# Decoder kernel, state-space stage: eight product buffers, scans five groups behind, one buffer of exponent rows loaded in halves, and block-step rows in place of the mask matmul

## Chip, core and metric

One core of one Trainium2 chip. The metric is the device time of the whole kernel in microseconds (us). TensorE is written PE, its weight loads PEld, VectorE DVE, ScalarE ACT, GpSimd POOL and SyncE SP.

## What is computed

A decoder of two layers on x of shape (4, 256, 256) runs in six stages, named A to F in the code: A attention, B a lookup of four experts by token, C a mixture of experts, D the state-space layer, E a second attention, F a second mixture of experts. The change touches stage D alone. With the projection, convolution and gate left out, D computes for each sequence b, each chunk of 128 tokens and each of 64 heads h:

```
dt    = softplus(A_log)
A_cum = cumsum(-dt) within the chunk
L[s, z]  = exp(A_cum[s] - A_cum[z])      for z <= s, else 0
Y_diag[s] = sum_z  (C[s] . B[z]) * L[s, z] * x[z]       8 numbers per head; C and B shared by 8 heads
Y_off     = what the state of the chunk before adds
out   = ((Y_diag + Y_off + D * x / dt) * silu(z_gate)) @ out_proj_w.T
```

## The kernel before

Every engine has its own program, and all five follow one list of steps that `schedule` writes out by hand; an engine skips the kinds of step in which it has no part. Inside an engine the order is fixed, and semaphores tie the engines together.

Stage D works in eight units (4 sequences times 2 chunks, variable `u`). A unit has 16 groups (`hg`, NHG = 16) of four heads each (HG = 4). For one group:

1. PE writes the exponents, 128 x 512 (four heads side by side, z on partitions and s along the row), into one of the three banks of ring AR: line 1450 multiplies the identity by the causal mask `maskt` (-1e30 where s < z), and line 1452 adds A_cum[s] - A_cum[z] by a product of 15 rows (`rows_z`, `rows_s`: each number is split into three bf16 parts).
2. ACT takes the exponential of the bank into a product buffer `M` (line 1055). There are NM = 4 buffers; ACT waits on `m_used` for the buffer to come free.
3. DVE multiplies the buffer by `CBs`, the C.B products, in place (line 1807).
4. PE scans: `scan` multiplies the buffer by the unit's x (line 1114, four matmuls of 32 columns side by side) into a bank of O. PE does this for the group LAG = 3 behind the one whose exponents it writes.

Between the groups the list places other work, by group number: projection of a pair of conv channels (`din`, PE line 1391, ACT lines 983 and 985) at groups 1, 4 and 9 while pairs are left (units 0 to 4), its three `tap` steps on DVE one group apart (line 1749), `th` on ACT (line 996, waits for the taps), `silu` on DVE (line 1759); for the last unit `y_t` (copy ACT 1066, transposes PE 1260, sums on DVE 1833 to 1839), `dy_t` (PE 1484, ACT 1071) and `dy` (PE 1490); for the next unit `at`, `dz` (PE 1397), `zs`, `xt` (PE 1428) and `cb` (PE 1437, DVE copies 1797). `state` stands at group 0. Bank T is one bank with one chain of waits: each user waits until the one before has been read; `at` and `dy_t` both use it.

The exponent rows of a unit come by DMA. At step `at` PE transposes the split sums (`ap_`, line 1418), ACT copies them into AT and, negated, nAT (lines 1030, 1031), and SP issues six DMAs (lines 697, 699) into one of two sets of `rows_s` / `rows_z`, one in the arena and one in `early`, memory that stages A and B used. Before it writes a set again, SP waits for the last group of the unit two back. PE waits for all six before a unit's first group.

Of the kernel before, what the change touches and what calls it, by code (L numbers as in the profile page):

```python
# [367 lines left out]
def decoder(nc, A, out, stages="ABCDEF"):  # L368
    steps = schedule(stages)
    at = number(steps)  # L370
    with ExitStack() as ctx:
# [135 lines left out]
        ap_ = cut(3 * NU * NV // 2, BF16).rearrange("p (u j m g) -> p u j m g", u=NU, j=HG, m=3)  # L507
# [4 lines left out]
        rows_s = [a.rearrange("p (j g s) -> p j g s", j=HG, g=NHG)  # L512
                  for a in (cut(RS, BF16, RR), early[0:RR, 0:RS].bitcast(BF16))]
        rows_z = [a.rearrange("p (g z) -> p g z", g=NHG)
                  for a in (cut(RZ, BF16, RR), early[0:RR, RS:RS + RZ].bitcast(BF16))]

# [9 lines left out]
        NM = 4  # L526
        M = cut(NM * 512).rearrange("p (c n) -> p c n", c=NM)
# [5 lines left out]
        t_a, t_abs, t_u, t_1u = (M[:, k, :] for k in range(4))  # L533
# [27 lines left out]
        ap_ready, decin_ready, dec_ready, rows_landed = sems("ap_ready decin_ready dec_ready rows_landed")  # L561
# [80 lines left out]
        def _(sp):  # L642
# [20 lines left out]
            for kind, s, i in steps:  # L663
                if kind == "m_t":
                    k = attn_index(s, i)

                    sp.wait_ge(t_read, at["T"]["m_t", s, i] + 1)

                    if k >= 2:
                        sp.wait_ge(pv_used, 8 * (k - 1))  # L670
                    for m in range(2):
                        sp.dma_start(QT[KQ + m:KQ + m + 1, k % 2, :, :],
                                     MT[m * NH:(m + 1) * NH, :]).then_inc(m_landed, 16)
                elif kind == "switch" and s == "D":
# [5 lines left out]
                    for c in range(2):  # L680
                        sp.dma_start(rows_s[c][3:RR, :, :, :], A["onehot"]).then_inc(hot_in, 16)
                        sp.dma_start(rows_z[c][0:3, :, :], A["ones3"]).then_inc(hot_in, 16)
# [160 lines left out]
        def _(act):  # L843
# [15 lines left out]
            for kind, s, i in steps:  # L859
# [164 lines left out]
                elif kind == "at":  # L1024
                    act.wait_ge(t_full, at["T"]["at", s, i] + 1)

                    if i:
                        act.wait_ge(rows_landed, 16 * 6 * i)
# [18 lines left out]
                elif kind == "ssd":  # L1047
# [7 lines left out]
                    a.activation(M[:, k % NM, :], AR[n % 3][:, :], ACT.Exp).then_inc(a_read, 1)  # L1055
# [18 lines left out]
        def _(pe):  # L1074
# [27 lines left out]
            def scan(s, u, hg):  # L1102

                k = NHG * u + hg
                if hg == 0:
                    bk = o_bank("ssd", s, u)

                    pe.wait_ge(xsp_ready, u + 1)
                pe.wait_ge(m_ready, k + 1)
                bk = O[at["O"]["ssd", s, u] % 2]  # L1110
                quarter, h = divmod(hg, HG)
                for j in range(HG):

                    ins = mm(bk[j * 32:(j + 1) * 32, quarter * P:(quarter + 1) * P],  # L1114
                             xsp[u % 2][:, quarter, h, j, :, :].rearrange("p q w -> p (q w)"),
                             M[:, k % NM, j * P:(j + 1) * P], start=(h == 0), stop=(h == HG - 1), skip_group_check=True)
                ins.then_inc(m_used, 1)

            pe.wait_ge(const_in, 64)
            for kind, s, i in steps:  # L1120
# [293 lines left out]
                elif kind == "at":  # L1414
                    bk = t_bank("at", s, i)
                    pe.wait_ge(ap_ready, 1)
                    for h in range(2):
                        ins = tr(bk[:, :].bitcast(BF16)[0:RA, h * P:(h + 1) * P],
                                 ap_[:, i, 2 * h:2 * h + 2, :, :].rearrange("p j m g -> p (j m g)"), identb[:, :])
# [21 lines left out]
                elif kind == "ssd":  # L1441
                    u, hg = i
                    if hg == 0:

                        if u == 0:
                            pe.wait_ge(hot_in, 64)
                        pe.wait_ge(rows_landed, 16 * 6 * (u + 1))
# [46 lines left out]
        def _(dve):  # L1494
# [10 lines left out]
            for kind, s, i in steps:  # L1505
# [276 lines left out]
                elif kind == "acum":  # L1782
# [5 lines left out]
                    cum, rest = (a.rearrange("p (u j g) -> p u j g", j=HG, g=NHG) for a in (t_a, t_rest))  # L1788
                    link(v.tensor_copy(ap_[:, :, :, 0, :], cum))
                    link(v.tensor_tensor(rest, cum, ap_[:, :, :, 0, :], ALU.subtract))  # L1790
                    link(v.tensor_copy(ap_[:, :, :, 1, :], rest))
                    v.tensor_tensor(ap_[:, :, :, 2, :], rest, ap_[:, :, :, 1, :], ALU.subtract).then_inc(ap_ready, 1)
                elif kind == "cb":
                    for par in range(2):
                        n = at["V"]["cb", s, i, par]
                        dve.wait_ge(v_full, n + 1)
                        v.tensor_copy(CBs[:, i % 2, par:NG:2, :], V[n % 2][:, :].rearrange("p (g s) -> p g s", g=NG // 2)
                                      ).then_inc(v_read, 1)
                elif kind == "ssd":
# [6 lines left out]
                    m = M[:, (NHG * u + hg) % NM, :].rearrange("p (h z) -> p h z", h=HG)  # L1806
                    v.tensor_tensor(m, m, CBs[:, u % 2, hg // (NV // NG):NG:NG // HG, :], ALU.mult).then_inc(m_ready, 1)  # L1807
# [38 lines left out]
def layouts(inp):  # L1846
# [62 lines left out]
    arrays["onehot"] = np.tile(np.repeat(np.eye(HG), 3, 0)[:, :, None, None], (1, 1, NHG, P)).astype(bf)  # L1909
# [16 lines left out]
```

## Time and profile before

| what | us |
|---|---|
| median of 3 runs | 1003.58 (995.57 to 1004.53) |
| span of the profiled execution, first to last instruction | 1004.2 |
| PE busy, share of span | 822.1, 82% |
| DVE busy | 584.5, 58% |
| ACT busy | 380.8, 38% |
| POOL busy | 221.1, 22% |
| the eight units of stage D, first mask matmul to the last unit's end | about 461 to 711 |
| mean granted clock of PE, whole span | 0.886 of 2.4 GHz |

The profiled execution has no other time than its span; it lies 0.6 us above the median of the runs. Busy shares are means over stages with different limits, so they say little about one stage. A granted clock of 1.00 in a window is 2.4 GHz, and 0.50 is 1.2 GHz; a value between them is a mix of both within the window. Durations of neighbouring instructions of one engine overlap in the trace, since each lasts from its start to the landing of its result; what one costs its engine is the distance from its start to the next one's.

### The profile page before, as it was taken

The numbers are of one execution on the slowest core, as the hardware profiler recorded it, in microseconds if no ns is written. First come the engines' busy times: TensorE is split into PE (matmuls) and PEld (weight loads), VectorE is DVE, ScalarE is ACT, GpSimd is POOL, SyncE is SP. The second block draws the span as 40 slices with busy tenths as digits, with TensorE's granted clock in tenths as the row PEclk, the third lists the DMA queues.
The fourth block names the chain that finished last, engine by engine and source line by source line (L and its number), as shares of the span: only waits on it lengthen the run. The fifth ranks groups of instructions, "written<-read, shape, count | busy, mean of one in ns | idle before, by whom it ended". The sixth has DMA issues, their size and how long they took to land.

```text
span 1004.2 us, 14716 instructions
## 1 busy us (share of the span) xinstructions
PE 822.1 (82%) x5680; PEld 530.7 (53%) x5680; DVE 584.5 (58%) x1184; ACT 380.8 (38%) x653; POOL 221.1 (22%) x210
## 2 busy tenths in 40 slices
PE   1678777599899799657899899999757777899998
PEld 0334443258677588523444444434434554677776
DVE  5765642544545457535787878547577663645443
ACT  1124334001444356244455445335213345444442
POOL 3200000123433322041110111001231111432432
PEclk9989878599899899866999999669578799799999
DMA  8000001000121211100000000000000001232231
GB/s 307 28 2 1 3 1 48 1 0 23 57 79 55 72 48 32 18 0 5 5 6 5 4 3 5 5 5 2 1 2 2 2 2 49 64 93 64 79 92 45
DMA packets 17669, 32.98 MB, mean 33 GB/s; under 512 B 5642, under 2 KB 9610, under 8 KB 17320
## 3 DMA queue, kind: packets, MB, share of 16 engines
q1 hardware_dynamic: 17600, 32.03, 10.4%
q8 instruction: 46, 0.75, 0.3%
q14 instruction: 23, 0.19, 0.1%
HBM read 30.06 MB, written 1.05 MB: 31 GB/s over the span
## 4 chain that ended last, share of the span: by engine, by line
PE 57%; DVE 21%; issue 11%; ACT 5%; POOL 4%; DMA 1%; SPq 0%; DVEq 0%; ACTq 0%; POOLq 0%
PE bank L1352 12%; PE bank L1376 8%; PE bank L1391 5%; PE bank L1299 3%; PE bank L1114 3%; PE bank L1452 2%; DVE s_arena L1807 2%; DVE s_xn L1523 2%; PE bank L1490 2%; PE bank L1314 2%; PE bank L1450 2%; DVE s_arena L1749 2%; PE bank L1243 2%; DVE s_arena L1595 2%; PE bank L1397 2%
## 5 line engine op out<-in xcount | busy, mean ns | idle before, releaser
L777 POOL TENSOR_TENSOR s_wl<-s_wmoe,s_wh 128x768 fp32r<-128x768 f32 x54 | 99.3, 1841 | 174.2 <-ACT s_wh L947 174.2
L1807 DVE TENSOR_TENSOR s_arena<-s_arena 128x512 f32<-128x512 f32 x128 | 89.8, 711 | 54.9 <-ACT s_arena L1055 54.5
L1055 ACT ACTIVATE s_arena<-bank 128x512 f32<-128x512 f32 x128 | 74.6, 602 | 74.8 <-PE bank L1452 74.8
L896 ACT ACTIVATE s_arena<-bank 128x512 f32<-128x512 f32 x96 | 56.6, 597 | 106.9 <-PE bank L1219 59.2
L1595 DVE TENSOR_REDUCE s_arena<-bank 128x2 f32<-128x512 f32 (+1 forms) x96 | 64.8, 687 | 35.0 <-PE bank L1190 18.6
L1714 DVE TENSOR_TENSOR s_act<-bank,s_sg_moe 128x512 f32<-128x512 f32 x54 | 37.4, 692 | 81.5 <-PE bank L1352 75.0
L1352 PE MATMUL bank<-s_xh,s_wh 128*128 128x512 f32 x216 | 73.2, 421 | 8.0 <-POOL s_wl L777 7.9
L959 ACT CAST s_ah<-s_act 128x512 fp32r<-128x512 f32 x54 | 33.6, 622 | 101.8 <-DVE s_act L1719 79.1
L1352 PE MATMUL bank<-s_xl,s_wh 128*128 128x512 f32 x216 | 69.4, 403 | 0.0
L1352 PE MATMUL bank<-s_xh,s_wl 128*128 128x512 f32 x216 | 69.2, 403 | 0.0
L1376 PE MATMUL bank<-s_wh,s_ah 128*128 128x256 f32 x216 | 66.5, 308 | 2.8 <-DVE s_al L1725 2.8
L1749 DVE SCALAR_TENSOR_TENSOR s_arena<-s_arena,s_convw 128x256 f32<-128x256 f32 x144 | 68.0, 513 | 0.6
L1376 PE MATMUL bank<-s_wl,s_ah 128*128 128x256 f32 x216 | 61.5, 285 | 0.0
L1376 PE MATMUL bank<-s_wh,s_al 128*128 128x256 f32 x216 | 61.5, 285 | 0.0
L1725 DVE TENSOR_TENSOR s_al<-s_act,s_ah 128x512 fp32r<-128x512 f32 x54 | 37.4, 692 | 40.3 <-ACT s_ah L959 40.2
L725 POOL TENSOR_TENSOR s_rstd<-s_ve,s_mhalf 128x2 f32<-128x2 f32 x24 | 16.6, 692 | 192.2 <-DVE s_ve L1515 192.1
L1450 PE MATMUL bank<-s_maskt,s_identb 128*128 128x512 bf16 x128 | 53.5, 418 | 5.5 <-issue 5.5
L1391 PE MATMUL bank<-s_xnT,s_win 128*128 128x256 f32 x192 | 53.5, 428 | 0.0
L1376 PEld LDWEIGHTS bank<-s_wh,s_ah 128*128 128x128 f32 x216 | 41.5, 192 | 13.4 <-issue 8.2
L1146 PE MATMUL bank<-s_ident,s_xn 128*128 128x128 f32 x80 | 15.7, 330 | 38.9 <-DVE s_xn L1523 36.7
L1352 PEld LDWEIGHTS bank<-s_xl,s_wh 128*128 128x128 f32 x216 | 42.3, 196 | 9.8
L1352 PEld LDWEIGHTS bank<-s_xh,s_wh 128*128 128x128 f32 x216 | 39.3, 198 | 15.5 <-DVE s_act L1714 7.0
(220 smaller groups left out, 1673.5 us busy)
## 6 DMA issues: line engine op xcount, KB each, us to landing
s_wmoe<-in_wF SPq DMA_DIRECT2D x28, 384.0 KB, 3.1
s_wmoe<-in_wC SPq DMA_DIRECT2D x26, 384.0 KB, 3.1
s_win<-in_win SPq DMA_DIRECT2D x1, 2112.0 KB, 10.5
s_x<-in_x SPq DMA_DIRECT2D x4, 256.0 KB, 3.5
s_early<-in_ctxT SPq DMA_DIRECT2D x1, 1024.0 KB, 9.5
s_ctxn<-in_ctx SPq DMA_DIRECT2D x1, 1024.0 KB, 12.4
out_x<-s_x SPq DMA_DIRECT2D x4, 256.0 KB, 2.9
s_xnT<-in_tok SPq DMA_DIRECT2D x1, 512.0 KB, 7.8
```

Source lines behind the costliest of these rows:

```text
L777: g.tensor_tensor(wl[:, w % NS_, :], wmoe[:, w % NW, :], wh[:, w % NS_, :], ALU.subtract).then_inc(wl_ready, 1)
L896: a.activation(PT[:, p % NPT, :], AR[n % 3][:, :], ACT.Exp).then_inc(a_read, 1)
L1055: a.activation(M[:, k % NM, :], AR[n % 3][:, :], ACT.Exp).then_inc(a_read, 1)
L1352: ins = mm(G[2 * (n % 2) + half][:, :], a_[:, k, half, :], b_[:, k, toks], start=(p_ == 0), stop=(p_ == len(parts) - 1))
L1376: ins = mm(Y[t // NT][:, (t % NT) * D:(t % NT + 1) * D], a_[:, w % NA, t * P:(t + 1) * P], b_[:, w % NS_, 2 * KD * P:], start=(j == 0 and ...
L1391: ins = mm(bk[:, h * L:(h + 1) * L], win[:, k, ct * P:(ct + 1) * P], xnT_of(s)[:, k, b * L:(b + 1) * L], start=(k == 0), stop=(k == KD - 1))
L1450: mm(bk[:, :], identb[:, :], maskt[:, :].unsqueeze(1).to_broadcast([P, HG, P]), start=True, stop=False, skip_group_check=True)
L1595: v.tensor_reduce(nM[:, q, h0:h0 + heads], V[n % 2][:, :].rearrange("p (h k) -> p h k", h=heads), AX.X, ALU.max, negate=True).then_inc(v_r ...
L1714: v.tensor_tensor(act_[:, w % 2, :], G[2 * (n % 2) + 1][:, :], sg_moe[:, n % 2, :], ALU.mult).then_inc(g_read, 1)
L1725: v.tensor_tensor(al[:, w % NA, :], act_[:, w % 2, :], ah[:, w % NA, :], ALU.subtract).then_inc(al_ready, 1)
L1749: ins = v.scalar_tensor_tensor(o, raw[:, m % NRAW, h, KS - 1 - k:KS - 1 - k + L], convw[:, ct, KS - 1 - k:KS - k], o, ALU.mult, ALU.add)
L1807: v.tensor_tensor(m, m, CBs[:, u % 2, hg // (NV // NG):NG:NG // HG, :], ALU.mult).then_inc(m_ready, 1)
```

## The change

- `NM` from 4 to 8 product buffers, the four new ones in `early`; `LAG` from 3 to 5, so PE scans five groups behind. `y_t`, `dy_t` and `dy` of the last unit move from groups 3, 5, 7 to 5, 7, 9; the places of the next unit's steps (at 6, dz 8, zs 10, xt 12, cb 13) stay.
- The mask matmul of line 1450 is gone. In its place the 15 exponent rows become 30: fifteen constant rows add -1e30 to whole blocks of 8 tokens that lie before the block of z. Inside the block of 8 the exponent of s < z is then not masked and may be positive. DVE therefore takes min(exp, 1) in the product (tensor_tensor becomes scalar_tensor_tensor), and the copy of the C.B products multiplies by -1 and by the triangle `tri`, which is -1 where z <= s and 0 elsewhere.
- One set of `rows_s` / `rows_z` in place of two. It is loaded in two halves of eight groups, five DMAs each (10 a unit in place of 6, of half the size). A half is loaded after the same half of the unit before has been used; PE waits for half 0 before group 0 and for half 1 before group 8. ACT waits for both halves of the last load before it writes AT again. The split of the sums on DVE is done in two halves, eight instructions for four.

```diff
-LAST_UNIT = (3, "y_t"), (5, "dy_t"), (7, "dy")
+LAST_UNIT = (5, "y_t"), (7, "dy_t"), (9, "dy")
-LAG = 3
-RR = 3 + 3 * HG
-RA = HG // 2 * 3 * NHG
+LAG = 5
+RL = 3 + 3 * HG
+STEPS = 16
+RR = RL + STEPS - 1
+GH = NHG // 2
+RA = HG * 3 * GH
...
-        NM = 4
+        NM = 8
+        M = [M4[:, c, :] if c < 4 else early[:, (c - 4) * 512:(c - 3) * 512] for c in range(NM)]
...
-                    if i >= 2:
-                        sp.wait_ge(a_full, at["A"]["ssd", s, i - 2, NHG - 1] + 1)
-                    for j in range(HG):
-                        h = 3 * NHG * (j % 2)
-                        sp.dma_start(rows_s[i % 2][0:3, j, :, :], AT[h:h + 3 * NHG, j // 2, :]).then_inc(rows_landed, 16)
-                    for h in range(2):
-                        sp.dma_start(rows_z[i % 2][3 + 6 * h:9 + 6 * h, :, :], nAT[:, h, :]).then_inc(rows_landed, 16)
+                    for half in range(2):
+                        if i:
+                            sp.wait_ge(a_full, at["A"]["ssd", s, i - 1, GH * (half + 1) - 1] + 1)
+                        gs_ = slice(GH * half, GH * half + GH)
+                        for j in range(HG):
+                            sp.dma_start(rows_s[0:3, j, gs_, :], AT[3 * GH * j:3 * GH * (j + 1), half, :]
+                                         ).then_inc(rows_landed[half], 16)
+                        sp.dma_start(rows_z[3:3 + 3 * HG, gs_, :], nAT[:, half, :]).then_inc(rows_landed[half], 16)
...
-                    mm(bk[:, :], identb[:, :], maskt[:, :].unsqueeze(1).to_broadcast([P, HG, P]),
-                       start=True, stop=False, skip_group_check=True)
-                    mm(bk[:, :], rows_z[u % 2][:, hg, :], rows_s[u % 2][:, :, hg, :], start=False, stop=True,
-                       skip_group_check=True).then_inc(a_full, 1)
+                    mm(bk[:, :], rows_z[:, hg, :], rows_s[:, :, hg, :], start=True, stop=True
+                       ).then_inc(a_full, 1)
...
-                        v.tensor_copy(CBs[:, i % 2, par:NG:2, :], V[n % 2][:, :].rearrange("p (g s) -> p g s", g=NG // 2)
-                                      ).then_inc(v_read, 1)
+                        v.scalar_tensor_tensor(CBs[:, i % 2, par:NG:2, :],
+                                               V[n % 2][:, :].rearrange("p (g s) -> p g s", g=NG // 2), -1.0,
+                                               tri[:, 0, :].unsqueeze(1).to_broadcast([P, NG // 2, P]),
+                                               ALU.mult, ALU.mult).then_inc(v_read, 1)
...
-                    v.tensor_tensor(m, m, CBs[:, u % 2, hg // (NV // NG):NG:NG // HG, :], ALU.mult).then_inc(m_ready, 1)
+                    v.scalar_tensor_tensor(m, m, 1.0, CBs[:, u % 2, hg // (NV // NG):NG:NG // HG, :], ALU.min, ALU.mult
+                                           ).then_inc(m_ready, 1)
...
+    step = P // STEPS * np.arange(1, STEPS)
+    before = np.where(i[None, :] < step[:, None], NEG, 0.0)
+    inside = (i[None, :] // (P // STEPS) == np.arange(1, STEPS)[:, None]).astype(np.float64)
+    arrays["onehot"] = np.concatenate([onehot, np.tile(before[:, None, None, :], (1, HG, NHG, 1))], 0).astype(bf)
+    arrays["blocks"] = np.tile(inside[:, None, :], (1, NHG, 1)).astype(bf)
```

## Rows read from the trace of the kernel before

**Rows 1.** Windows, one per unit: PE, PEld, DVE, ACT, POOL busy, granted clock, DMA.
```profile
461.00:490.20 29.20, 28.68 (x204) 13.68 (x203) 19.54 (x37) 15.47 (x32) 3.51 (x5) 0.86 0.02 5
490.20:523.60 33.40, 30.98 (x246) 16.52 (x246) 25.19 (x52) 17.61 (x37) 4.46 (x6) 0.95 0.02 4
523.60:555.50 31.90, 28.93 (x250) 14.88 (x250) 26.09 (x47) 17.93 (x38) 3.78 (x6) 1.00 0.02 4
555.50:590.30 34.80, 30.73 (x248) 16.47 (x246) 27.84 (x60) 18.23 (x38) 5.45 (x7) 0.95 0.02 4
590.30:622.90 32.60, 30.42 (x250) 15.76 (x245) 25.20 (x47) 17.02 (x35) 3.52 (x5) 0.95 0.02 4
622.90:655.00 32.10, 30.56 (x218) 13.61 (x222) 20.45 (x43) 13.04 (x25) 4.21 (x7) 0.73 0.02 4
655.00:686.50 31.50, 30.60 (x226) 12.84 (x222) 16.40 (x25) 12.65 (x24) 2.50 (x5) 0.73 0.02 4
686.50:711.00 24.50, 20.82 (x182) 8.39 (x174) 20.48 (x51) 10.33 (x18) 2.99 (x5) 0.87 0.01 2
```

**Rows 2.** Waits, 461 to 712 us: total us, times, longest.
```profile
ACT s_arena L1055 <- PE bank L1452: 74.8, 61, 6.0
DVE s_arena L1807 <- ACT s_arena L1055: 54.5, 42, 5.0
...
ACT s_arena L996 <- DVE s_arena L1749: 20.5, 10, 3.4
...
PEld bank L1114 <- DVE s_arena L1807: 14.8, 29, 2.2
...
PE bank L1260 <- ACT s_arena L1066: 7.5, 6, 2.0
```

**Rows 3.** Timeline of TensorE, one step at full clock: start, us, instruction.
```profile
646.25 0.39 PE L1450 MATMUL bank<-s_maskt,s_identb 128*128 128x512 bf16 x1
646.57 0.38 PE L1452 MATMUL bank<-s_early 15*128 15x512 bf16 x1
646.89 0.43 PE L1114 MATMUL bank<-s_arena,s_wmoe 128*32 128x128 f32 x8
647.25 0.39 PE L1450 MATMUL bank<-s_maskt,s_identb 128*128 128x512 bf16 x1
```

**Rows 4.** Timeline of TensorE, one step at half clock.
```profile
630.55 0.63 PE L1450 MATMUL bank<-s_maskt,s_identb 128*128 128x512 bf16 x1
631.12 0.60 PE L1452 MATMUL bank<-s_early 15*128 15x512 bf16 x1
631.65 0.66 PE L1114 MATMUL bank<-s_arena,s_wmoe 128*32 128x128 f32 x8
632.24 0.61 PE L1450 MATMUL bank<-s_maskt,s_identb 128*128 128x512 bf16 x1
```

**Rows 5.** Groups by line, VectorE, 461 to 711 us: count, busy, mean ns, idle before.
```profile
L1807 DVE TENSOR_TENSOR s_arena<-s_arena 128x512 f32<-128x512 f32 x126 | 88.6, 712 | 54.9 <-ACT s_arena L1055 54.5
L1749 DVE SCALAR_TENSOR_TENSOR s_arena<-s_arena,s_convw 128x256 f32<-128x256 f32 x90 | 43.9, 528 | 0.0
```

**Rows 6.** Timeline of VectorE from 526 us.
```profile
526.14 0.68 DVE L1759 SCALAR_TENSOR_TENSOR s_arena<-s_arena 128x512 f32<-128x512 f32 x1
526.74 1.88 DVE L1807 TENSOR_TENSOR s_arena<-s_arena 128x512 f32<-128x512 f32 x3
```

**Rows 7.** Chain that ended last, before the first unit: start, us, what.
```profile
455.41 5.49 issue
```

**Rows 8.** Timeline of SyncE's queue: issues for the first unit.
```profile
454.42 3.13 SPq L697 DMA_DIRECT2D s_arena<-s_arena  x4
457.60 1.61 SPq L699 DMA_DIRECT2D s_arena<-s_arena  x2
```

**Rows 9.** Windows of 2 us, columns as in rows 1: two pauses of TensorE.
```profile
658.00:660.00 2.00, 1.10 (x12) 0.48 (x12) 1.39 (x2) 1.25 (x3) 0.00 (x0) 1.00 0.00 0
...
564.00:566.00 2.00, 0.07 (x1) 0.10 (x2) 1.15 (x3) 1.78 (x4) 0.00 (x0) 1.00 0.01 4
```

More of the change, by code:

```diff
@@ L506, in decoder @@
         dec = cut(NU * NV)
-        ap_ = cut(3 * NU * NV // 2, BF16).rearrange("p (u j m g) -> p u j m g", u=NU, j=HG, m=3)
+        ap_ = cut(3 * NU * NV // 2, BF16).rearrange("p (u i j m g) -> p u i j m g", u=NU, i=2, j=HG, m=3)
         AT = cut(2 * P // 2, BF16, RA).rearrange("p (i s) -> p i s", i=2)
@@ L511, in decoder @@
         RS, RZ = NHG * HG * P // 2, NHG * P // 2
[L512 to L515, printed above, removed]
+        rows_s = cut(RS, BF16, RR).rearrange("p (j g s) -> p j g s", j=HG, g=NHG)
+        rows_z = cut(RZ, BF16, RR).rearrange("p (g z) -> p g z", g=NHG)
         XS = NHG * P
@@ L531, in decoder @@
         yfT = ys.rearrange("p (k q) -> p k q", k=DI // P)
-        t_a, t_abs, t_u, t_1u = (M[:, k, :] for k in range(4))
+        t_a, t_abs, t_u, t_1u = M[0:4]
         t_max, t_rest = yf, yo
@@ L560, in decoder @@
             "zs_ready nab_ready u_ready w_ready ln_ready dt_ready")
-        ap_ready, decin_ready, dec_ready, rows_landed = sems("ap_ready decin_ready dec_ready rows_landed")
+        ap_ready, decin_ready, dec_ready = sems("ap_ready decin_ready dec_ready")
+        rows_landed = [sem(f"rows_landed{i}") for i in range(2)]
         xsp_ready = sem("xsp_ready")
@@ L679, in _ @@
                     sp.wait_ge(ctx_in, 32)
-                    for c in range(2):
-                        sp.dma_start(rows_s[c][3:RR, :, :, :], A["onehot"]).then_inc(hot_in, 16)
-                        sp.dma_start(rows_z[c][0:3, :, :], A["ones3"]).then_inc(hot_in, 16)
+                    sp.dma_start(rows_s[3:RR, :, :, :], A["onehot"]).then_inc(hot_in, 16)
+                    sp.dma_start(rows_z[0:3, :, :], A["ones3"]).then_inc(hot_in, 16)
+                    sp.dma_start(rows_z[RL:RR, :, :], A["blocks"]).then_inc(hot_in, 16)
                 elif kind == "moe" and i[1] < SHARED[s] + ROUTED:
@@ L1027, in _ @@
                     if i:
-                        act.wait_ge(rows_landed, 16 * 6 * i)
+                        act.wait_ge(rows_landed[0], 16 * 5 * i)
+                        act.wait_ge(rows_landed[1], 16 * 5 * i)
                     src = T[:, :].bitcast(BF16)[0:RA, 0:2 * P].rearrange("p (i s) -> p i s", i=2)
@@ L1054, in _ @@
                         act.wait_ge(m_used, k - NM + 1)
-                    a.activation(M[:, k % NM, :], AR[n % 3][:, :], ACT.Exp).then_inc(a_read, 1)
+                    a.activation(M[k % NM], AR[n % 3][:, :], ACT.Exp).then_inc(a_read, 1)
                 elif kind == "state" and i % 2 == 0:
@@ L1115, in scan @@
                              xsp[u % 2][:, quarter, h, j, :, :].rearrange("p q w -> p (q w)"),
-                             M[:, k % NM, j * P:(j + 1) * P], start=(h == 0), stop=(h == HG - 1), skip_group_check=True)
+                             M[k % NM][:, j * P:(j + 1) * P], start=(h == 0), stop=(h == HG - 1), skip_group_check=True)
                 ins.then_inc(m_used, 1)
@@ L1418, in _ @@
                         ins = tr(bk[:, :].bitcast(BF16)[0:RA, h * P:(h + 1) * P],
-                                 ap_[:, i, 2 * h:2 * h + 2, :, :].rearrange("p j m g -> p (j m g)"), identb[:, :])
+                                 ap_[:, i, h, :, :, :].rearrange("p j m g -> p (j m g)"), identb[:, :])
                     ins.then_inc(t_full, 1)
@@ L1442, in _ @@
                     u, hg = i
[L1443 to L1447, printed above, removed]
+                    if hg % GH == 0:
+                        if u == 0 and hg == 0:
+                            pe.wait_ge(hot_in, 48)
+                        pe.wait_ge(rows_landed[hg // GH], 16 * 5 * (u + 1))
                     bk = a_bank("ssd", s, u, hg)
-                    mm(bk[:, :], identb[:, :], maskt[:, :].unsqueeze(1).to_broadcast([P, HG, P]),
-                       start=True, stop=False, skip_group_check=True)
-                    mm(bk[:, :], rows_z[u % 2][:, hg, :], rows_s[u % 2][:, :, hg, :], start=False, stop=True,
-                       skip_group_check=True).then_inc(a_full, 1)
+                    mm(bk[:, :], rows_z[:, hg, :], rows_s[:, :, hg, :], start=True, stop=True
+                       ).then_inc(a_full, 1)
                     k = NHG * u + hg - LAG
@@ L1787, in _ @@
                     v.tensor_copy(d3[:, :, 1], cum[:, :, 1]).then_inc(decin_ready, 1)
[L1788 to L1792, printed above, removed]
+                    cum, rest = (a.rearrange("p (u j i g) -> p u i j g", j=HG, i=2, g=GH) for a in (t_a, t_rest))
+                    for h in range(2):
+                        ins = v.tensor_copy(ap_[:, :, h, :, 0, :], cum[:, :, h])
+                    link(ins)
+                    for h in range(2):
+                        ins = v.tensor_tensor(rest[:, :, h], cum[:, :, h], ap_[:, :, h, :, 0, :], ALU.subtract)
+                    link(ins)
+                    for h in range(2):
+                        ins = v.tensor_copy(ap_[:, :, h, :, 1, :], rest[:, :, h])
+                    link(ins)
+                    for h in range(2):
+                        ins = v.tensor_tensor(ap_[:, :, h, :, 2, :], rest[:, :, h], ap_[:, :, h, :, 1, :], ALU.subtract)
+                    ins.then_inc(ap_ready, 1)
                 elif kind == "cb":
```

6 lines of the change are left out of this document (3 added, 3 removed).

## Prediction, made before the changed kernel ran

> **What bounds the kernel now.** Only stage D changes, so I asked for windows first, one per unit [rows 1]. A unit of the first five takes 29.2 to 34.8 us; PE is busy 28.7 to 31.0 of them, DVE 25.2 to 27.8 (19.5 in unit 0), ACT 15 to 18, POOL under 6. Units 5 and 6 have no projections left (DVE 20.5 and 16.4), yet last as long: the granted clock is 0.73, so PE spent (1 - 0.73) x 2 = 54% of them at 1.2 GHz. In unit 7 DVE (20.5) and PE (20.8) are level in 24.5 us. So PE leads everywhere, with DVE close behind in units 1 to 4 and 7.
>
> Next, the waits say who is late [rows 2]. ACT waits 74.8 us for the exponents and DVE 54.5 us for ACT: both come from PE's lateness. The other way, PE's scans wait 14.8 us for DVE's product, and its transposes at y_t 7.5 us (6 times, 1.25 each) for ACT's copy. ACT also waits 20.5 us for DVE's taps.
>
> Last, the timeline of one step, for what each part costs PE. At 2.4 GHz the mask starts at 646.25, the rows' product at 646.57, the scan at 646.89, the next mask at 647.25: 0.32 + 0.32 + 0.36 = 1.00 us [rows 3]. At 1.2 GHz it is 0.57 + 0.53 + 0.59 = 1.69 us [rows 4].
>
> **The change part by part.** *Mask matmul out.* It takes 0.32 us of PE per group, 0.57 us at the low clock, and a step becomes 0.68 or 1.12 us [rows 3, 4]. The product with 30 rows in place of 15 costs nothing: the mask with 128 rows lasts 0.39 us, the product with 15 rows 0.38 [rows 3], and 30 lies between. So 16 x 0.32 = 5.1 us of PE leave a unit at full clock.
> The Trainium skill (TensorE: Matmul & The Clock Gate, section Back-to-back issue gap) gives N/2.4 + 2.5 ns for a warm matmul, 216 ns for 512 columns. By that figure the 128 masks would be worth 27.6 us, and by the row's distance of 0.32 us they are worth 41; I go by the trace, in which each matmul here also has its own weights.
>
> *What DVE lets through.* The products are 88.6 and the taps 43.9 of DVE's busy us in the stage [rows 5]; the change leaves their number and sizes as they are. Three products in a row take 1.88 us, so one costs 0.60, and the scalar_tensor_tensor of the same size ahead of them starts 0.60 before them [rows 6]; that one too reads two f32 tiles of SBUF. So the new form costs nothing. The C.B copies, also 128 x 512, cost the same by that row; between zero and 0.1 us each, 2 a unit. In units 1 to 4 DVE is busy 25.2 + 26.1 + 27.8 + 25.2 = 104.3 us and PE 31.0 + 28.9 + 30.7 + 30.4 = 121.0, of which 4 x 5.1 = 20.4 go: 100.6. The two are then level, and DVE becomes the bound by a little. Neither can work through: ACT's tanh waits for the taps of the group before [rows 2], and that keeps ACT, whatever LAG and NM say, within about a group of DVE three times a unit. Between 100% (104 us) and DVE's present 79% (132.7 us) I take 92%, because PE now waits for DVE only with five groups between them and the four units' idle DVE time was PE's lateness: 104.3 / 0.92 = 113.4, a gain of 132.7 - 113.4 = **19.3 us**.
>
> *Unit 0*: 29.2 us, PE busy 28.7, DVE 19.5 and thus no bound: 16 masks, a few at the low clock, 5.1 to 6; some of it lost to the filling of the longer pipeline: **5.0**.
>
> *Units 5 and 6*: DVE and ACT (13) are far below. In each, about 6 masks lie in the low stretch: 6 x 0.57 + 10 x 0.32 = 6.6. PE stays the bound, so nearly all of it shows. The ACT copy at y_t keeps its length while the steps that hide it shrink by 0.3, and the same holds for the chain at dy_t: I take off 0.8 a unit. 2 x 5.8 = **11.6**.
>
> *Unit 7*: 24.5 us with DVE busy 20.5. At 93% DVE takes 22: **2.5**.
>
> *LAG 5 and eight buffers* have no term of their own: they are why the bubble at a unit's change (PE's wait for DVE, 14.8 us in 29 waits [rows 2]) can go. What is late next is DVE itself.
>
> *Moved steps.* y_t, dy_t, dy move two groups, as does the scan they follow, so their distance from it is unchanged. New is that `at` (6) now comes before dy_t (7) on bank T: PE's dy_t waits for ACT's two copies of AT, and behind it on PE wait the rows of group 8. Before it was the reverse, `at` waiting for dy_t's copy. Zero to 0.5 us a unit, in units where PE leads; within the 0.8 above. dz and dy now lie one group apart.
>
> *Rows in halves.* Six issues take 3.13 + 1.61 = 4.7 us [rows 8], 0.8 each; ten take 7.8 at that price, or 4.7 if the price goes with size. SP has nothing else to issue in this stage. In the first unit PE waits 5.5 us, to 460.9 [rows 7], 1.7 us after the last issue ended (459.2). With half 0 alone it waits for five issues: 0.8 us less. The eight half-size split instructions on DVE for four stand ahead of it, 4 x 0.2 = 0.8 more; together zero, plus or minus 1. Later, half 1 of a unit is issued when group 15 of the unit before has its exponents, and lands at most 5 x 0.8 + 1.7 = 5.7 us later. PE needs it 8 groups on (over 8 x 0.68 = 5.4, plus state, y_t and projections): covered. ACT's wait at the next `at`, 6 groups on, is closer: in units 1 to 4 the two projections before it cover it; in units 5 and 6 it has 7 x 0.68 + about 2 for state and y_t = 6.8. If that cover goes, all of ACT's exponentials are queued behind it, and then DVE and PE: up to 1 us, twice.
>
> **Sum.** 19.3 + 5.0 + 11.6 + 2.5 = 38.4 off 1004.2, which stands 0.6 above the median of the runs: **966 us** (-3.8%).
>
> **Rivals.**
> *DVE takes PE's place and is used no better.* For: th ties ACT to the taps, DVE's order is fixed, and din, taps and sums come in bursts. Against: the 54.5 us that DVE idles is time in which PE was late. If DVE stays at 80% in units 1 to 4, they take 131 us (1.7 off); with 3 off unit 0, 11.6 off units 5 and 6 and 1 off unit 7 it is 17: **987**.
>
> *The clock, on the slow side.* After 658 to 660 us, in which PE was busy 1.10 of 2 us, the clock fell to 1.2 GHz, while after 564 to 566, busy 0.07, it did not [rows 9]; and while PE ran steps without a pause at 631 to 632 it stayed low [rows 4]. So steps of this kind don't bring the clock back by themselves, and the change takes from them their fullest matmul and leaves PE more pauses behind DVE. A unit in the low clock takes 24.9 (PE's full-clock work) x 1.7 = 42 us against 33 now and 28 forecast: it decides from (33 - 28) / (42 - 28) = a third of the time of units 0 to 4 at 1.2 GHz. At half the time there, 5 x 35 = 175 for 162 now, and units 5 to 7 no faster: +13, **1017**. Against: in units 1 to 4 the clock was 0.95 to 1.00 with pauses in it, and the projections (f32) stay.
>
> *The new DVE form is slow.* The Trainium skill (Vector Engine (DVE) Microarchitecture Reference, section 7, Points that are easy to get wrong) says that this form with two non-bf16 SBUF sources halves throughput.
> As a mechanism here: 16 x 0.6 = 9.6 us more DVE per unit, 35.7 in units 1 to 4, at 93% 38.4 against 33.2: +21; with +5 in unit 7 and nothing gained elsewhere, **1030**. The row of 0.60 for such an instruction [rows 6] speaks plainly against it.
>
> *Better than forecast.* DVE near 97% and, with dz and dy close together, a shorter low stretch in units 5 and 6 (they lose 17 us each to it now, of which five could come back each): 6 + 10 more: **950**.
>
> **Chances.** Forecast (956 to 977) 0.55; DVE no better used (977 to 993) 0.20; better (under 956) 0.12; gain eaten up, within 1% of now, 0.06; clock 0.05; slow form 0.02. One per cent (10 us) is about what this kernel's runs can tell from no change, since three of them span 9 us. The range, 950 to 990, leaves out about 0.06 below and 0.14 above, and takes in the bounds of the small terms (about 3 us). Faster by over 1%: 0.87; within 1%: 0.06; slower: 0.07.
>
> **What would show it.** Right: units 1 to 4 at about 28 us with DVE busy over 90%; ACT's wait for the exponents well under 74.8 us; steps without other work 0.68 us apart; PE's wait for scans moved to "behind DVE" but short; product 0.60 to 0.69 us. Wrong: granted clock in units 1 to 4 under 0.85; products over 1 us; waits of ACT or PE for the row DMAs; DVE idle over 4 us a unit, ended by ACT.

## The result, and the profile after

The changed kernel takes 1007.2 us (median of 20 runs, 1002.06 to 1011.32) against 1003.96 us (20 runs): 1.0041 times as long, 95% interval 1.0023 to 1.0059. Forecast were 966 us. The 41 us of matmuls are gone from the program, and the time is no shorter. The profiled execution has a span of 1006.2 us and a mean granted clock of 0.862, where before it had 1004.2 and 0.886.

First the whole stage, from the first product of a unit to the last residual sum, in one window for each kernel (columns as in rows 1). Before:

```profile
460.90:723.40 262.50, 240.21 (x1850) 117.00 (x1850) 185.10 (x360) 123.60 (x239) 30.41 (x45) 0.86 0.02 4
```

After:

```profile
459.10:722.10 263.00, 229.17 (x1722) 115.19 (x1722) 184.46 (x360) 123.05 (x239) 31.83 (x46) 0.75 0.02 4
```

It lasts as long as before (263.0 us for 262.5), with 128 matmuls fewer (1722 for 1850). DVE's and ACT's work is the same to a microsecond. PE is busy 11.0 us less, where the removed matmuls alone took at least 128 x 0.32 = 41, the price at full clock; its pauses rose from 22.3 to 33.8 us. The clock says where the rest went: from 0.86 to 0.75, so the time at 1.2 GHz rose from 2 x 0.14 x 262.5 = 74 us to 132. By unit it answers to [rows 1] like this:

```profile
459.10:487.40 28.30, 26.39 (x171) 12.92 (x171) 17.27 (x33) 14.84 (x30) 2.95 (x5) 0.72 0.02 4
487.40:526.80 39.40, 34.05 (x234) 17.56 (x230) 25.80 (x55) 17.82 (x35) 4.13 (x7) 0.74 0.02 4
526.80:560.40 33.60, 28.77 (x231) 15.18 (x227) 25.26 (x45) 17.41 (x35) 4.29 (x6) 0.85 0.02 4
560.40:598.60 38.20, 32.61 (x235) 17.59 (x231) 27.88 (x62) 17.71 (x35) 4.92 (x8) 0.78 0.02 4
598.60:632.10 33.50, 28.66 (x230) 15.12 (x227) 25.17 (x45) 17.44 (x35) 4.21 (x6) 0.85 0.02 4
632.10:661.80 29.70, 26.09 (x211) 12.31 (x207) 21.54 (x46) 13.57 (x26) 4.95 (x9) 0.71 0.02 4
661.80:684.70 22.90, 21.29 (x206) 9.89 (x202) 16.06 (x25) 12.14 (x24) 3.11 (x6) 0.85 0.03 6
684.70:712.00 27.30, 25.18 (x220) 10.64 (x216) 23.36 (x55) 10.95 (x19) 3.27 (x6) 0.60 0.01 3
```

Units 1 to 4 had clocks of 0.95 to 1.00 and now have 0.74 to 0.85; they take 144.7 us for 132.7. Units 5 and 6 gained 11.0 us (52.6 for 63.6), unit 0 0.9, and unit 7 lost 2.8; what is left behind unit 7 takes 10.1 us for 12.4. How the clock falls is to be seen at the change to unit 1 in PE's timeline:

```profile
486.04 0.38 PE L1456 MATMUL bank<-s_arena 30*128 30x512 bf16 x1
486.35 0.42 PE L1120 MATMUL bank<-s_arena 128*32 128x128 f32 x8
486.71 0.38 PE L1456 MATMUL bank<-s_arena 30*128 30x512 bf16 x1
487.02 0.43 PE L1120 MATMUL bank<-s_arena 128*32 128x128 f32 x8
487.38 0.39 PE L1456 MATMUL bank<-s_arena 30*128 30x512 bf16 x1
487.70 0.42 PE L1120 MATMUL bank<-s_arena 128*32 128x128 f32 x8
491.07 1.14 PE L1480 MATMUL bank<-s_arena 64*128 64x64 f32 x16 [2.94 <-DVE s_arena L1809]
492.14 0.60 PE L1456 MATMUL bank<-s_arena 30*128 30x512 bf16 x1
492.67 0.66 PE L1120 MATMUL bank<-s_early,s_arena 128*32 128x128 f32 x8
493.26 3.78 PE L1397 MATMUL bank<-s_xnT,s_win 128*128 128x256 f32 x8
496.97 0.60 PE L1456 MATMUL bank<-s_arena 30*128 30x512 bf16 x1
497.51 0.66 PE L1120 MATMUL bank<-s_early,s_arena 128*32 128x128 f32 x8
498.09 0.60 PE L1456 MATMUL bank<-s_arena 30*128 30x512 bf16 x1
```

A step costs 0.67 us at full clock (486.04 to 486.71), as forecast. PE then waits 2.94 us for DVE's C.B products (line 1809), and from 492 on the same step costs 1.12 us and a projection 3.71 (493.26 to 496.97) in place of the 1.93 of the one at 479.18 us, at full clock. The waits in the stage, for [rows 2]:

```profile
DVE s_arena L1821 <- ACT s_arena L1061: 41.1, 26, 4.2
ACT s_arena L1061 <- PE bank L1456: 40.4, 21, 4.4
ACT s_arena L988 <- PE bank L1397: 40.1, 15, 3.7
...
ACT s_early L1061 <- PE bank L1456: 14.4, 17, 1.8
```

ACT waits for exponents 40.4 + 14.4 = 54.8 us in place of 74.8, but 12.7 us more for projections, which the low clock stretches: 40.1 us, where before it was

```profile
ACT s_arena L983 <- PE bank L1391: 27.4, 14, 3.5
```

DVE's product keeps its price in the new form, with the buffers in `early` and in the arena:

```profile
L1821 DVE SCALAR_TENSOR_TENSOR s_early<-s_early,s_arena 128x512 f32<-128x512 f32 x64 | 46.0, 730 | 4.4 <-ACT s_early L1061 4.4
...
L1821 DVE SCALAR_TENSOR_TENSOR s_arena<-s_arena 128x512 f32<-128x512 f32 x64 | 43.4, 687 | 41.1 <-ACT s_arena L1061 41.1
```

730 and 687 ns, for 712 before [rows 5]; PE and ACT nowhere wait for a row DMA after the first unit, and in the first PE waits 4.5 us in place of 5.5 [rows 7]. PE's scans now wait 0.6 us for DVE's products.

### The profile page after: what moved, and what is told of

Same layout as the page of the kernel before. It is cut to its first block, busy times and chain, and to the rows that moved or that the text cites. A ratio compares the mean times of both kernels' runs of the same rounds, so it can differ in the third digit from the quotient of the medians.

```text
span 1006.2 us, 14500 instructions
## 1 busy us (share of the span) xinstructions
PE 806.9 (80%) x5552; PEld 526.8 (52%) x5552; DVE 583.9 (58%) x1188; ACT 380.5 (38%) x653; POOL 221.7 (22%) x210
## 4 chain that ended last, share of the span: by engine, by line
PE 60%; DVE 20%; issue 10%; ACT 5%; POOL 4%; DMA 1%; SPq 0%; DVEq 0%; ACTq 0%; POOLq 0%
PE bank L1358 13%; PE bank L1382 7%; PE bank L1397 5%; PE bank L1120 4%; PE bank L1456 3%; PE bank L1305 3%; PE bank L1403 3%; DVE s_xn L1527 2%; PE bank L1320 2%; PE bank L1494 2%; PE bank L1249 2%; DVE s_arena L1599 2%; POOL s_rstd L730 1%; PE bank L1192 1%; DVE s_arena L1753 1%
## 5 line engine op out<-in xcount | busy, mean ns | idle before, releaser
L901 ACT ACTIVATE s_arena<-bank 128x512 f32<-128x512 f32 x96 | 56.7, 597 | 108.8 <-PE bank L1225 58.6
L964 ACT CAST s_ah<-s_act 128x512 fp32r<-128x512 f32 x54 | 33.6, 622 | 101.9 <-DVE s_act L1723 79.3
L1821 DVE SCALAR_TENSOR_TENSOR s_arena<-s_arena 128x512 f32<-128x512 f32 x64 | 43.4, 687 | 41.1 <-ACT s_arena L1061 41.1
L1456 PE MATMUL bank<-s_arena 30*128 30x512 bf16 x128 | 58.6, 459 | 8.0 <-issue 4.5
L1729 DVE TENSOR_TENSOR s_al<-s_act,s_ah 128x512 fp32r<-128x512 f32 x54 | 37.4, 692 | 40.3 <-ACT s_ah L964 40.2
L1397 PE MATMUL bank<-s_xnT,s_win 128*128 128x256 f32 x192 | 56.7, 447 | 0.1
L1061 ACT ACTIVATE s_arena<-bank 128x512 f32<-128x512 f32 x64 | 37.9, 602 | 40.8 <-PE bank L1456 40.4
L988 ACT ACTIVATE s_arena<-bank,s_convw 128x256 f32<-128x256 f32 x48 | 24.5, 561 | 66.1 <-PE bank L1397 66.1
L1821 DVE SCALAR_TENSOR_TENSOR s_early<-s_early,s_arena 128x512 f32<-128x512 f32 x64 | 46.0, 730 | 4.4 <-ACT s_early L1061 4.4
```

Source lines behind the costliest of these rows:

```text
L901: a.activation(PT[:, p % NPT, :], AR[n % 3][:, :], ACT.Exp).then_inc(a_read, 1)
L1061: a.activation(M[k % NM], AR[n % 3][:, :], ACT.Exp).then_inc(a_read, 1)
L1397: ins = mm(bk[:, h * L:(h + 1) * L], win[:, k, ct * P:(ct + 1) * P], xnT_of(s)[:, k, b * L:(b + 1) * L], start=(k == 0), stop=(k == KD - 1))
L1456: mm(bk[:, :], rows_z[:, hg, :], rows_s[:, :, hg, :], start=True, stop=True).then_inc(a_full, 1)
L1729: v.tensor_tensor(al[:, w % NA, :], act_[:, w % 2, :], ah[:, w % NA, :], ALU.subtract).then_inc(al_ready, 1)
L1821: v.scalar_tensor_tensor(m, m, 1.0, CBs[:, u % 2, hg // (NV // NG):NG:NG // HG, :], ALU.min, ALU.mult).then_inc(m_ready, 1)
```

## The experiments

Theory A: the mask matmul was what held PE's clock up, and without it the time it took is given back at 1.2 GHz. Rivals: B, DVE sets the pace and the clock only follows PE's pauses behind it; C, the later scans, the buffers or the loads cost what the mask gave. Each group of runs below was compared with the kernel before on its own chip. Stage times, clocks and time at 1.2 GHz are those of the profiled execution, from its first product to the last sum of the stage. "Low" is short for time at 1.2 GHz, worked out as 2 x (1 - granted clock) x length, as above.

**Putting the mask matmul back, in all groups or some.** The three runs differ from the changed kernel in this, with `fill` true always (e1_mask_back), for `hg >= 10 or hg == 0` (e3_fill_late) or for `0 < hg < 10` (e4_fill_early):

```diff
-                    mm(bk[:, :], rows_z[:, hg, :], rows_s[:, :, hg, :], start=True, stop=True
-                       ).then_inc(a_full, 1)
+                    if fill:
+                        mm(bk[:, :], identb[:, :], maskt[:, :].unsqueeze(1).to_broadcast([P, HG, P]),
+                           start=True, stop=False, skip_group_check=True)
+                    mm(bk[:, :], rows_z[:, hg, :], rows_s[:, :, hg, :], start=not fill, stop=True,
+                       skip_group_check=True).then_inc(a_full, 1)
```

> The changed kernel with the mask matmul put back in front of the product of 30 rows in every group (its result is added in, as before); LAG, buffers and halved loads stay as changed. Theory A (the removed matmul was what held TensorE's clock up, so that the 41 us it took are given back at 1.2 GHz): time 995 to 1007 us, granted clock of the stage back from 0.76 to 0.86 or more, stage about 250 us. Theory B (VectorE sets the pace, the clock only follows its pauses): TensorE's extra matmuls fall into the pauses and cost nothing, 1003 to 1009 us, with the clock a little higher. Theory C (the moved steps, the later scans or the halved loads cost what the mask gave): 1035 us or more, since the mask's 41 us come back on top.

> The changed kernel with the mask matmul put back in groups 10 to 15 and 0 only, seven of sixteen, where the trace of the changed kernel shows VectorE busy without a gap and TensorE pausing. Theory A together with the pauses (the clock falls where TensorE pauses at the change of units): the clock falls in fewer units, 0.82 to 0.90 in the stage, time 980 to 995 us. Theory B: TensorE's pauses are filled, VectorE still sets the pace: 1004 to 1009 us. Theory C: as the changed kernel plus 56 x 0.32 = 18 us, 1025.

> The changed kernel with the mask matmul put back in groups 1 to 9 only, nine of sixteen, where TensorE has the projections and leads. Theory A if only the amount of TensorE's work counts: much like the run with groups 10 to 15 and 0, 980 to 1000 us. Theory A together with the pauses: nothing is filled where the pause is, the clock still falls at the change of units, and the matmuls cost 0.57 us each in the low stretch: 1015 to 1035 us, clock 0.74 to 0.80. Theory B: 1007 to 1020 us.

Measured: e1 997.18 us, 0.990 of before (0.984 to 0.996), stage 250.5 us, 45 us of it at 1.2 GHz. e3 1009.52 us, 1.000 (0.996 to 1.004), stage 263.7, 116 us low. e4 997.64 us, 0.992 (0.989 to 0.995), stage 256.3, 72 us low. The window of e1's stage stands beside the one of after above:

```profile
458.30:708.80 250.50, 228.23 (x1850) 113.65 (x1850) 184.82 (x360) 123.88 (x239) 31.18 (x46) 0.91 0.02 4
```

Columns: length, PE, PEld, DVE, ACT, POOL busy, granted clock, DMA. With 128 matmuls more PE is busy 228.2 us, in place of 229.2: they cost nothing, since the clock is 0.91 in place of 0.75. C falls, since the time went down and not up by the mask's 41 us; A stands. The other two went against what I expected of the pauses. In e3 the matmuls stand in the groups where PE pauses behind DVE: they filled pauses (23.8 us for 33.8) and held little of the clock (116 us low for 132), where a gain to 980 to 995 us was expected. In e4 they stand in groups 1 to 9, between projections, where a loss to 1015 us or more was expected if the pauses counted. The kernel takes as long as e1 (997.64 and 997.18 us), though its profiled stage lies between (256.3 us, between 263.0 and 250.5): what the program does behind the stage took 5.3 us less in e4's profile than in e1's (280.9 and 286.2 us), a spread that is seen over all kernels here and is taken up at the end of the next section. How much of e1's gain lies in which groups is settled no closer than that.

**The mask part alone, on the kernel before.** Block-step rows in both sets, min and triangle on DVE, and

```diff
-                    mm(bk[:, :], identb[:, :], maskt[:, :].unsqueeze(1).to_broadcast([P, HG, P]),
-                       start=True, stop=False, skip_group_check=True)
-                    mm(bk[:, :], rows_z[u % 2][:, hg, :], rows_s[u % 2][:, :, hg, :], start=False, stop=True,
-                       skip_group_check=True).then_inc(a_full, 1)
+                    mm(bk[:, :], rows_z[u % 2][:, hg, :], rows_s[u % 2][:, :, hg, :], start=True, stop=True
+                       ).then_inc(a_full, 1)
```

> The kernel before with the mask part of the change alone: block-step rows in both sets, no mask matmul, min and triangle on VectorE; LAG 3, four buffers, two sets of rows, loads whole. Theory A: the clock falls as in the changed kernel (0.74 to 0.80 in the stage) and the time is 1000 to 1010 us. Theory B: the same time, but here the pauses of TensorE behind VectorE are longer, 1005 to 1015. Theory C: what was lost to LAG, buffers and loads is not lost here: 965 to 975 us.

Measured: 1004.1 us, 0.998 (0.995 to 1.002):

```profile
459.20:715.30 256.10, 219.74 (x1722) 114.47 (x1722) 184.28 (x359) 122.16 (x239) 31.02 (x45) 0.79 0.02 4
```

The stage has 108 us low, before 74. So the mask part by itself brings the low clock, and no gain in the kernel's time; the stage is 6.4 us shorter than before. It is also 6.9 us shorter than in the changed kernel (263.0 us, 132 low). The later scans and the rest of the change therefore gave nothing on top: with them the clock was lower still.

**The same time on PE with fewer rows.** The product of 30 rows is issued twice, the second overwriting the first:

```diff
+                    mm(bk[:, :], rows_z[:, hg, :], rows_s[:, :, hg, :], start=True, stop=True)
                     mm(bk[:, :], rows_z[:, hg, :], rows_s[:, :, hg, :], start=True, stop=True
                        ).then_inc(a_full, 1)
```

> The changed kernel with the product of 30 rows issued twice into the same bank in every group (the second overwrites the first): the same number of matmuls, the same 0.32 us each as with the mask matmul put back (997 us, clock 0.90), but 30 rows of the array in place of 128. If it is the time for which TensorE is occupied that holds the clock: 994 to 1002 us, mean clock 0.89 or more. If a matmul of few rows doesn't count as a full one: the clock stays at or under 0.86 and the time rises over the changed kernel's by up to 128 x 0.32 to 0.57 = 41 to 70 us, most likely 1020 to 1050 us.

Measured: 1029.42 us, 1.032 (1.024 to 1.040), clock 0.858.

```profile
456.50:737.20 280.70, 259.87 (x1850) 119.53 (x1850) 185.29 (x359) 124.18 (x239) 31.65 (x46) 0.76 0.02 4
```

The same number of matmuls as in e1 (1850), of the same 512 columns and type, and PE is busy 31.6 us longer, at 0.76 in place of 0.91. What PE is occupied with matters, and not only that it is occupied.

**The pause at the change of units.** The C.B products of the next unit stand at group 11 in place of 13, so that DVE has them done when PE comes to the state step; alone (e6), with the mask back in groups 1 to 9 (e7) and in all (e8):

```diff
-NEXT_UNIT = (6, "at"), (8, "dz"), (10, "zs"), (12, "xt"), (13, "cb")
+NEXT_UNIT = (6, "at"), (8, "dz"), (10, "zs"), (12, "xt"), (11, "cb")
```

> The changed kernel with the C.B products of the next unit two groups earlier (group 11 in place of 13), so that TensorE's state step at the change of units finds its bank read and doesn't pause 2.9 us there; amount of work unchanged. If the pause at the change of units brings the clock down: fewer falls, mean clock 0.88, 985 to 998 us. If the clock falls for want of full matmuls in the state-space steps whatever the pauses: 1002 to 1009 us with the clock still near 0.86.

> The same with the mask matmul also put back in groups 1 to 9. If pause and want of full matmuls both count: 980 to 992 us, mean clock 0.90 or more. If the pause doesn't count: as with groups 1 to 9 alone, 995 to 1000 us.

> The same with the mask matmul put back in every group: the highest clock of the three, 0.91 or more. If both count: 985 to 994 us, better than the 997 us of the same with the products at 13. If only the matmuls count: 995 to 1000 us.

Measured: e6 1007.03 us, 1.007 (1.003 to 1.012), clock 0.856; e7 1002.17 us, 1.001 (0.998 to 1.004), 0.879; e8 1008.19 us, 1.008 (1.005 to 1.011), 0.886. In e6 PE's wait at the state step shrank from 8.8 us to 1.7:

```profile
PE bank L1456 <- ACT s_early L1061: 5.7, 5, 1.5
...
PE bank L1480 <- DVE s_arena L1809: 1.7, 3, 0.6
```

and yet the stage has 131 us at 1.2 GHz, as the changed kernel (132). So this pause alone doesn't decide how low the clock is; PE still has 35.6 us of pauses in the stage. Both runs with the mask back came out slower than expected (980 to 1000 us). The move itself costs time there: by the medians 5 us (e7 against e4) and 11 (e8 against e1), by the ratios, each to the kernel before on its own chip, 9 and 18, and by the profiled stages 2 and 10 (258.2 and 260.6 us for 256.3 and 250.5). What became later in its place (the first row above, PE's wait for ACT to read an AR bank, is one candidate) was not tried.

**The product over 128 rows.** If few rows are the trouble, rows can be had for nothing: the product of 15 rows takes the same 0.32 us as the mask's of 128 [rows 3]. RR becomes 128; the added 98 rows are zeros in both operands (e9), or ones in `rows_z` and +1, -1 by turns in `rows_s` (e10):

```diff
-RR = RL + STEPS - 1
+RR = P
...
+    more = P - RL - STEPS + 1
+    fill_s, fill_z = np.zeros(more), 0.0
...
-    arrays["onehot"] = np.concatenate([onehot, np.tile(before[:, None, None, :], (1, HG, NHG, 1))], 0).astype(bf)
-    arrays["blocks"] = np.tile(inside[:, None, :], (1, NHG, 1)).astype(bf)
+    arrays["onehot"] = np.concatenate([onehot, np.tile(before[:, None, None, :], (1, HG, NHG, 1)),
+                                       np.tile(fill_s[:, None, None, None], (1, HG, NHG, P))], 0).astype(bf)
+    arrays["blocks"] = np.tile(np.concatenate([inside, np.full((more, P), fill_z)], 0)[:, None, :], (1, NHG, 1)).astype(bf)
```

> The changed kernel with its product of 30 rows widened to 128: rows 30 to 127 are zeros in both operands, loaded once with the constants. Result and number of matmuls are unchanged. If it is the number of rows that a matmul drives that holds the clock: mean clock 0.89 or more, and since no matmul is added, the saving of 0.32 us per group shows: 960 to 978 us. If zeros don't count (only rows that carry values do): as the changed kernel, 1003 to 1010 us, clock 0.86.

> The same with ones in the added rows of the one operand and +1, -1 by turns in those of the other, so that they add up to nothing. If values count and not only rows: 960 to 978 us with mean clock 0.89 or more even where the zeros fail; if rows count, the same as with zeros; if neither (the stationary operand must change, or the mask matmul helped by something else): 1003 to 1010 us.

Measured: e9 978.84 us, 0.979 (0.972 to 0.985); e10 980.89 us, 0.980 (0.974 to 0.986). Both beat the kernel before and the changed one. The stage of e9, which runs the changed kernel's instructions one for one:

```profile
458.80:692.20 233.40, 191.49 (x1722) 104.68 (x1722) 183.24 (x359) 121.65 (x239) 31.77 (x46) 0.89 0.02 4
```

1722 matmuls in both, and PE is busy 191.5 us in place of 229.2, at 0.89 in place of 0.75. PE's waits for the C.B products at the state step are 8.8 us in e9 as in the changed kernel, and DVE's instructions are the same. So the clock is what was given back, by an edit that adds no work to any engine, and B falls. A becomes narrower: what the mask matmul did for the clock, 128 rows in the product do as well.

The traces also say in what way. In units 1 to 4 of the changed kernel the clock fell eight times and was low for 58 us; three of these stretches last 10 us each. In e9 it fell six times and was low for 24 us, at most 7 at a stretch; in the kernel before three times, 10 us in all. Each of these falls came a few microseconds after a pause of PE, but not every pause was followed by one [rows 9]. At the change to unit 1 both kernels have the same pause (2.94 us, in e9 2.92) and then a fall, at 492.0 us in the one and 488.2 in the other. The changed kernel then stays low until 502.2, and e9 only until 491.6. So the pauses of PE have a part in the falls, and the wide product made the low stretches shorter here more than it made them fewer. Whether it is the rows in the loaded operand or those in the streamed one that count, no run tells: both were widened together.

**What the rest of the change is worth with the wide product.** The mask part alone with the wide product (e11), the same with zeros for the ones and with the second set's constants loaded behind the first unit's rows (e12), and e9 with the C.B products at 11 (e13) or with this (e14):

```diff
-LAST_UNIT = (5, "y_t"), (7, "dy_t"), (9, "dy")
-LAG = 5
+LAST_UNIT = (3, "y_t"), (5, "dy_t"), (7, "dy")
+LAG = 3
```

> The kernel before with the mask part of the change alone (LAG 3, four buffers, two whole sets of rows), and the product widened to 128 rows with +1 and -1. If the clock is held: what LAG, buffers and halved loads are worth once the clock doesn't hide it is the distance to the run before this one. With four buffers and LAG 3 TensorE must pause behind VectorE more: 970 to 988 us, against 960 to 978.

> The kernel before with the mask part alone (LAG 3, four buffers, two whole sets of rows) and the product widened to 128 rows with zeros, as two runs ago with +1 and -1, but the constants of the second set are loaded behind the first unit's rows, so that the first unit doesn't wait the 31 us for them that the trace of that run showed. If LAG, buffers and halves are worth the 7 us that remain of that run's distance once the 26 us of waiting are taken off: 983 to 990 us. If the mask part with a held clock is all: 976 to 982.

> The changed kernel with the product widened to 128 rows with zeros (978.8 us) and the C.B products of the next unit at group 11 in place of 13. With the clock mostly held, TensorE's pauses of 2.9 us at the change of units (8.8 us in three) are on the path now: 968 to 976 us. If the other pauses of TensorE grow in their place, as they did without the wide product: 977 to 985.

> The changed kernel with the product widened to 128 rows with zeros, but with LAG 3 and the last unit's steps at groups 3, 5 and 7 again; eight buffers and halved loads stay. If the five groups between exponents and scan are what LAG, buffers and halves are worth: 984 to 990 us, the same as the mask part alone. If the order of the last unit's steps or the loads are: 976 to 982.

Measured: e11 1012.92 us, 1.011 (1.004 to 1.017), of which its first unit waits 31.4 us for constants, 5.0 MB in two sets; a cost of my edit, and the reason that it lies outside what was expected. e12 994.15 us, 0.992 (0.989 to 0.994). e13 983.85, 0.984 (0.979 to 0.988): PE's wait at the state step is 2.5 us for 8.8, and that is no gain here either: the stage takes 239.6 us, and the time fits the second of the two expectations, that other pauses grow in its place. e14 989.29, 0.989 (0.985 to 0.994), stage 242.8 us for e9's 233.4. e12 still waits for the second set, 10.8 us at its longest:

```profile
PE bank L1122 <- DVE s_arena L1817: 17.0, 13, 3.1
PE bank L1460 <- issue: 16.2, 2, 10.8
```

Without those 10.8 its stage (252.4) is 241.6, as e14's 242.8 and as e11's 243.0 counted from where its wait ends. The timed medians put e12 less 10.8 at 983.4 us, 6 under e14, but of that 5.0 stand behind the stage (280.8 us for 285.8). So going from LAG 3 to LAG 5, with the last unit's steps behind it, is worth 9 us of the stage with the wide product, and the buffers and halved loads nothing that shows there. At LAG 3 PE waits 17.0 us for the products before its scans in e12, the first row above, and 12.8 + 5.7 in e14; in e9, at LAG 5, 4.0 + 0.9:

```profile
PE bank L1120 <- DVE s_early L1821: 12.8, 10, 2.4
...
PE bank L1120 <- DVE s_arena L1821: 5.7, 4, 3.1
```

These 13.6 us are not the gain, though. The stage of e14 reads

```profile
458.70:701.50 242.80, 199.35 (x1722) 108.19 (x1722) 183.92 (x359) 122.08 (x239) 31.78 (x46) 0.85 0.02 4
```

Beside e9 its pauses together are only 1.5 us longer (43.4 and 41.9 us). The other 7.9 of the 9.4 us are PE busy for longer (199.4 and 191.5 us) with the same 1722 matmuls, at 0.85 in place of 0.89: 73 us low for 51. The worth of the later scans thus shows almost wholly as clock, and with the 30-row product the sign was the other way: e2 has 108 us low and the changed kernel 132. Why LAG 5 goes with the higher clock in the one case and the lower in the other is open; LAG and the eight buffers were not tried apart from each other otherwise, nor any LAG above 5.

## Why the prediction was wrong

**The step that failed** is "Mask matmul out": that 5.1 us of PE leave a unit at full clock. The price of the matmul was right, its absence was not free. With it gone, the stage spent 132 us at 1.2 GHz in place of 74, and PE's busy time fell by 11.0 us in place of 41. The rival on the clock was the right mechanism and got 0.05. Its point of decision, a third of the time of units 0 to 4 at 1.2 GHz, holds: unit 0 spent 2 x 0.28 x 28.3 = 16 us there and units 1 to 4 2 x (0.26 x 39.4 + 0.15 x 33.6 + 0.22 x 38.2 + 0.15 x 33.5) = 57, together 73 of 173 us, 42%. By that rival's prices a unit then takes 28 + 0.42 x 14 = 34 us and the five 169; they took 173, 11 us more than before. What I had against it, that these units had their clock with pauses in them [rows 1, 9], no longer held once the matmul was gone.

**Units 5 and 6** were to give 11.6 us, 5.8 each, and gave 11.0. That the sum fits is partly luck: unit 5 gave 2.4, with its clock at 0.71, and unit 6 8.6, with its clock up from 0.73 to 0.85. **Unit 0** was to give 5.0 and gave 0.9: over half of it ran at 1.2 GHz; in e9 (clock 0.88) it took 24.1 us, which is the forecast.

**DVE at 92% in units 1 to 4** was too high by itself. In e9, with the clock mostly held, the same units, and 5 to 7 behind them, read

```profile
482.90:515.10 32.20, 26.13 (x234) 15.40 (x230) 25.55 (x55) 17.53 (x35) 4.09 (x7) 0.95 0.02 4
515.10:546.10 31.00, 26.69 (x230) 14.85 (x226) 25.09 (x45) 17.20 (x35) 4.33 (x6) 0.89 0.02 4
546.10:581.00 34.90, 29.07 (x235) 16.86 (x231) 27.73 (x62) 17.53 (x35) 4.88 (x8) 0.85 0.02 4
581.00:610.50 29.50, 24.98 (x231) 13.95 (x227) 25.17 (x45) 17.20 (x35) 4.32 (x6) 0.94 0.02 5
610.50:636.40 25.90, 21.49 (x210) 10.55 (x206) 21.21 (x45) 13.47 (x26) 4.79 (x9) 0.87 0.02 5
636.40:656.40 20.00, 17.88 (x206) 8.98 (x202) 16.12 (x25) 12.14 (x24) 3.16 (x6) 1.00 0.03 7
656.40:684.00 27.60, 18.80 (x224) 8.94 (x220) 23.26 (x55) 11.38 (x20) 3.35 (x6) 0.92 0.01 3
```

127.6 us with DVE busy 103.5, 81%: the first rival's figure (80%, 131 us). The forecast 19.3 us are 5.1 here. ACT waits 26.9 us for the taps in e9, as that rival had it. Units 5 and 6 gave 17.7 us there in place of 11.6: the mask is gone and their clock rose from 0.73 to 0.87 and 1.00, the "better" case in part.

**Unit 7** was to give 2.5 us and seems to have lost 3 in both kernels, with DVE's work up from 20.5 to 23.3. Most of that is where the stage is cut: in the kernel before four of DVE's products stand behind 711.0 us, in the changed one none behind 712.0. Unit 7 together with what follows it took 36.9 us before, 37.4 in the changed kernel and 35.8 in e9.

**What LAG 5 was to remove** was read wrongly. The 14.8 us of [rows 2] are the wait of PE's weight loads (PEld), which overlap its matmuls. The scans themselves waited less:

```profile
PE bank L1114 <- DVE s_arena L1807: 6.7, 8, 1.9
```

That wait did go, to 0.6 us, but other pauses took its place and more, so that PE's pauses in the stage rose from 22.3 to 33.8 us.

**The small terms** held. The new DVE form costs nothing against the old one: 687 and 730 ns in line 1821, where tensor_tensor took 712, and 0.60 us from start to start at 557.63, 558.23 and 558.83 us, as in [rows 6]. The Trainium skill (Vector Engine (DVE) Microarchitecture Reference, Points that are easy to get wrong) says that this form with two non-bf16 SBUF sources halves throughput. Measured against tensor_tensor of the same size that is not so here; whether both run at half of some faster rate, no run shows. The ten issues were always hidden; the moved steps were tried only together with LAG, so their own cost is not known.

**Outside the stage** the changed kernel is 3.3 us longer (284.1 us from the last sum to the end, before 280.8), more than the 2.0 us by which its whole profile is: the stage is 0.5 us longer and starts 1.8 us earlier. That part of the program was not edited in any run, and took 280.8 to 286.9 us in the sixteen profiled executions, without a pattern by edit; the cause stays open. A gain in the stage therefore shows in the kernel's time only to within about 6 us.

## What to carry to other kernels

Before a matmul is taken out of a stretch that TensorE leads, look at what the rest of the stretch is made of. Here mostly products over few rows and scans 32 columns wide were left, and the engine spent half of the stage at half clock and gave the whole gain back; so read the granted clock by windows before and after. A product over few rows can be widened to 128 with zero rows at no cost in its time. Here that one edit of constants was worth 28 us by the medians (1007.2 and 978.84 us) and 25 by the ratios (1.004 and 0.979). The deeper lag between producer and consumer was worth 9 us of the stage with the wide product (e9 and e14) and minus 7 without it (the changed kernel and e2), and both mostly by the clock: what an edit of the order is worth can turn around once the clock is mended, so measure it again then, and read PE's busy time for the same matmuls beside its pauses.

## What was not expected of the hardware

Rows of zeros counted: with 98 zero rows in both operands the stage had 51 us at 1.2 GHz, with 98 rows of ones against +1 and -1 also 51, and with 30 rows 132. The duration of the matmul did not depend on the rows (0.38 to 0.39 us at full clock with 15, 30 and 128). And work without a pause did not by itself bring the clock back: in the changed kernel it fell at about 468 us, in the middle of a projection, and stayed at 1.2 GHz to about 478 us, through four steps of a 30-row product and a scan, two transposes and four matmuls of 128 rows and 512 columns, with PE busy throughout. The first steps:

```profile
470.03 0.60 PE L1456 MATMUL bank<-s_arena 30*128 30x512 bf16 x1
470.56 0.66 PE L1120 MATMUL bank<-s_arena 128*32 128x128 f32 x8
471.15 0.60 PE L1456 MATMUL bank<-s_arena 30*128 30x512 bf16 x1
471.68 0.66 PE L1120 MATMUL bank<-s_arena 128*32 128x128 f32 x8
```
